# One VectorE instruction for two units: the multiplication by B in a selective scan, 1024 elements against 2048

## What is computed

```
x_dbl = einsum('bld,ed->ble', x, x_proj_w)
delta_r, B, C = x_dbl[..., :128], x_dbl[..., 128:144], x_dbl[..., 144:]
delta = softplus(einsum('blr,dr->bld', delta_r, dt_proj_w) + dt_proj_b)
A = -exp(A_log)
dA  = exp(delta[..., None] * A)                       # 512 channels, 16 states
dBu = (delta * u)[..., None] * B[:, :, None, :]
h   = dA_t * h + dBu_t                                # over 64 tokens, from zero
y_t = einsum('bdn,bn->bd', h, C_t)
y + u * D
```

## Time and profile before

| | |
|---|---|
| median of 3 runs | 1930.55 us (1928.92 to 1934.46) |
| the profiled execution | 1929.09 us, span 1927.3 us |
| VectorE busy | 1456.1 us, 76% of the span |
| TensorE busy | 1832.9 us, 95% |
| GpSimd busy | 1266.2 us, 66% |
| ScalarE busy | 1261.0 us, 65% |
| the scan, L996 | x256, 581.8 us, mean 2273 ns |
| the multiplication by B, L927 | x256, 151.7 + 151.6 us, mean 1194 ns |
| first scan, last scan | 33.5 us, 899.4 us after the span's start |

### The profile page before, as it was taken

The page is one execution under the profiler, slowest core; times in us unless marked ns, Lnnn a source line. Parts: engine busy times, 40 slices in busy tenths (PEclk is TensorE's granted clock), DMA queues, the critical chain, the costliest instruction groups (busy, mean ns, idle before and its releaser), DMA issues.

```text
span 1927.3 us, 30225 instructions
## 1 busy us (share of the span) xinstructions
PE 1832.9 (95%) x9439; PEld 1276.3 (66%) x9439; DVE 1456.1 (76%) x2572; ACT 1261.0 (65%) x3937; POOL 1266.2 (66%) x1251
## 2 busy tenths in 40 slices
PE   6899999999999999988599899999999999999998
PEld 6777777777777777755355575756667575665765
DVE  8999999999999999997545564655657566565522
ACT  5888888888888888765355564655647465564621
POOL 5789999999999999988676554544545454450000
PEclk9999999999999999999799999999999999999999
DMA  5423332333233332321776334334343433431021
GB/s 204 152 105 145 144 117 107 139 145 133 101 128 145 144 122 102 126 88 40 216 213 187 110 102 124 104 107 127 104 119 106 116 109 111 124 91 54 30 71 34
DMA packets 133198, 228.59 MB, mean 119 GB/s; under 512 B 31076, under 2 KB 86388, under 8 KB 128048
## 3 DMA queue, kind: packets, MB, share of 16 engines
q1 hardware_dynamic: 99952, 161.38, 24.0%
q0 software_dynamic: 33088, 65.28, 12.5%
HBM read 209.99 MB, written 44.70 MB: 132 GB/s over the span
## 4 chain that ended last, share of the span: by engine, by line
PE 47%; ACT 2%; issue 1%; DMA 1%; DVE 1%; POOL 0%; DVEq 0%; SPq 0%; ACTq 0%; POOLq 0%
PE attn_psum L1906 12%; PE attn_psum L1922 11%; PE attn_psum L1825 5%; PE attn_psum L1838 5%; PE attn_psum L1818 5%; PE attn_psum L1864 3%; PE attn_psum L1809 2%; PE attn_psum L1940 2%; PE attn_psum L1799 1%; PE attn_psum L1850 1%; ACT xh L1551 1%; ACT th L1552 1%; DMA kv_at<-kv_scratch,new_now 0%; ACT prob L1509 0%; ACT k_t L1499 0%
## 5 line engine op out<-in xcount | busy, mean ns | idle before, releaser
L996 DVE TENSOR_TENSOR_SCAN hid<-scan_psum,dbu 128x1024 f32<-128x1024 f32 x256 | 581.8, 2273 | 0.0
L1161 PE MATMUL scan_psum<-hid,ident 128*128 128x256 f32 x2048 | 519.8, 384 | 28.8 <-POOL hid L492 28.6
L1161 PEld LDWEIGHTS scan_psum<-hid,ident 128*128 128x128 f32 x2048 | 377.9, 190 | 192.0 <-issue 106.4
L1660 DVE CUSTOM_DVE_ANT_0 prob<-attn_psum,mask 128x336 f32<-128x336 f32 x256 | 120.1, 505 | 287.2 <-PE attn_psum L1818 286.8
L492 POOL TENSOR_TENSOR hid<-hid,kv_at 128x1024 f32<-128x1024 f32 x128 | 306.2, 2405 | 27.5 <-DVE hid L996 27.1
L492 POOL TENSOR_TENSOR hid<-hid,bc 128x1024 f32<-128x1024 f32 x128 | 306.0, 2403 | 23.1 <-DVE hid L996 22.8
L1515 ACT COPY p_t<-attn_psum 112x384 f32<-112x384 f32 x256 | 122.3, 484 | 291.6 <-PE attn_psum L1825 291.6
L1922 PE MATMUL attn_psum<-w,ffn_hid 128*128 128x512 f32 x512 | 238.9, 596 | 5.0 <-DVE y_sb L1725 5.0
L1443 POOL DMA_INDIRECT kv_at<-kv_scratch,new_now x189 | 200.5, 1061 | 64.1 <-issue 57.1
L1906 PE MATMUL attn_psum<-xs_in,w 128*128 128x256 f32 x1024 | 232.6, 381 | 7.5 <-ACT xs_in L1521 6.6
L635 ACT ACTIVATE scan_psum<-kv_at,neg_a 128x252 f32<-128x252 f32 x512 | 211.6, 465 | 13.9 <-DVE hid L996 12.3
(11 more groups left out here) (221 smaller groups left out, 3038.7 us busy)
## 6 DMA issues: line engine op xcount, KB each, us to landing
bc<-bc_scratch SPq DMA_DIRECT2D x16, 2048.0 KB, 7.5
kv_at<-bc_scratch SPq DMA_DIRECT2D x15, 2048.0 KB, 7.2
q_scratch<-qg SPq DMA_DIRECT2D x32, 260.0 KB, 2.0
early<-q_scratch SPq DMA_DIRECT2D x32, 260.0 KB, 3.1
x_pair<-in_x_pairs SPq DMA_DIRECT2D x32, 256.0 KB, 2.7
kv_scratch<-kvg SPq DMA_DIRECT2D x32, 256.0 KB, 2.1
a_scratch<-a_sb SPq DMA_DIRECT2D x32, 256.0 KB, 3.4
w_o<-x_scratch SPq DMA_DIRECT2D x32, 256.0 KB, 3.2
```

The source lines that it names most:

```text
L996: nc.vector.tensor_tensor_scan(hid[:, k % RING, :, :].rearrange("p n t -> p (n t)"), decay[k % 2], dbu[:, k % RING, :, :].rearrange("p n t ...
L1161: mm = nc.tensor.matmul(yc, ident[:], hid[:, k % RING, i, :], start=False, stop=(k % 4 == 3 and i == 3))
```

## The change

`times_b` takes a number of units, two by default: one instruction multiplies `du` by the B of 8 states, 2048 elements in each partition, into two neighbouring buffers of the ring. The first two units of all still have an instruction each. In a quarter the order on VectorE becomes: scan 0, multiplication 2 and 3, scan 1, scan 2, multiplication 4 and 5, scan 3, scan 4, multiplication 6 and 7, scan 5, `prepare`, scan 6, multiplication 0 and 1 of the next quarter, scan 7.

```diff
-            def times_b(t, h, q, k):
+            def times_b(t, h, q, k, units=2):
...
-                wait(dve, dve_h, e + 1 - RING)
-                nc.vector.tensor_tensor(dbu[:, k % RING, :, :], du[:, c % 2, :].unsqueeze(1).to_broadcast([P, 4, SUB]),
-                                        bc[q // 2][:, 4 * j:4 * j + 4, 0, :], ALU.mult).then_inc(dve_dbu, 1)
+                wait(dve, dve_h, e + units - RING)
+                nc.vector.tensor_tensor(
+                    dbu[:, k % RING:k % RING + units, :, :].rearrange("p r n t -> p (r n) t"),
+                    du[:, c % 2, :].unsqueeze(1).to_broadcast([P, 4 * units, SUB]),
+                    bc[q // 2][:, 4 * j:4 * (j + units), 0, :], ALU.mult).then_inc(dve_dbu, units)
...
                 for k in range(8):
+                    if k == 6 and parts.next_scan:
+                        prepare(*after)
+                    if s == 0 and k == 0:
+                        times_b(t, h, q, 1, 1)
+                    if k % 2 and k < 7 and parts.scan:
+                        times_b(t, h, q, k + 1)
                     if k == 7 and parts.next_scan:
-                        prepare(*after)
-                    if k < 7 and parts.scan:
-                        times_b(t, h, q, k + 1)
+                        times_b(*after, 0)
...
-                    if k == 7 and parts.next_scan:
-                        times_b(*after, 0)
...
-            times_b(0, 0, 0, 0)
+            times_b(0, 0, 0, 0, 1)
```

## The result

| | before | changed |
|---|---|---|
| median | 1930.92 us, 19 runs | 1935.95 us, 19 runs |
| lowest to highest | 1928.79 to 1934.46 | 1933.11 to 1938.21 |
| changed over before | | 1.0023, 95% interval 1.0016 to 1.0029 |
| the profiled execution's span | 1927.3 us | 1933.8 us |
| first and last scan start | 33.5, 899.4 us | 33.7, 903.4 us |

What follows compares the result with a forecast made beforehand. VectorE and a chain through GpSimd, TensorE and ScalarE were both taken as critical. Terms +5.4, −1.3, −0.15 and +0.9 sum to +4.85; 1930.55 + 4.8 gives 1935.3 us, range 1929.5 to 1939.5.

Steps and rivals of the forecast that it cites:

- the case that was forecast: Scan stage: GpSimd, TensorE and ScalarE delay scan 0 in every second quarter; 1935.3 us, own range 1932.5 to 1938, chance 0.65.
- The sum of 4.85: Whole kernel: +5.4 for twelve pairs of quarters, −1.3 and −0.15 for other quarters, +0.9 for the second quarter.
- The merge: VectorE: a merged multiplication of 2048 elements occupies 2.18 us instead of 2.24, 7.0 us less work over 127 instructions.
- rivals B: VectorE's multiplications: the chain binds and merging saves nothing, spacing 2.23; 1938.8 us, chance 0.10.
- C: VectorE's multiplications: the fixed part is the whole 0.12 us, spacing 2.11; 1930.8 us, no change, chance 0.10.
- The chain: From scan 5 through GpSimd, TensorE and ScalarE to scan 0 two quarters on: 0.56 us later, +0.45 per two quarters.
- The stall of unit 6: Before scan 6: its exponentials come behind `add_bias`, some 0.7 us later, stalling VectorE by up to 0.3, not counted.
- The second quarter: `prepare` waits 3.78 us for GpSimd's `step`, which stands behind unit 5; one-time cost +0.9 us.
- The sentence that what lies behind the scans only starts later: Stages behind the scans: they start later and are unchanged, no cost of their own.
- Rival A: Scan stage: the chain does not bind, under 53.8 us in two quarters, VectorE's saving comes through; 1924.7 us, chance 0.12.
- Rival D: `prepare` meets GpSimd at work in every quarter, up to 2.17 us each; 1993 us, chance 0.03.

Runs made afterwards that it cites:

- order only: Changed kernel with each merged multiplication split into two single ones of 1024 elements, new order kept: 1938.40 us, 1.0037 of the kernel before.
- the tables: Changed kernel with GpSimd's two key tables behind unit 4 instead of unit 5: 1932.34 us, 1.0005 of the kernel before.
- the lock: Changed kernel with `prepare` reading delta alone, without the multiplication by u: 1931.52 us, 1.0002 of the kernel before.
- the copy of q: Changed kernel with ScalarE's exponentials of the next quarter's unit 0 ahead of its copy of q: 1933.24 us, 1.0007 of the kernel before.
- tables and exponentials moved: Changed kernel with key tables behind unit 4 and exponentials of unit 0 ahead of ScalarE's q copy: 1931.26 us, 0.9997 of the kernel before.
- the old order with nearly the same edits: Kernel before with key tables behind unit 4 (to 28th quarter), unit 0's exponentials before q copy, early quarters' second `step` behind unit 3: 1927.40 us.

## Why the prediction was right

The ratio, 1.0023, or 4.5 us, is close to the forecast loss of 4.8, and the case that was forecast is the one that came, by its own rows. That the totals are so close is in part luck. The sum of 4.85 was all in the scan stage, and there the loss was 3.9. Outside it, in the two profiles, stood 0.9 that the prediction had put at nothing: 0.2 ahead of the first scan and 0.7 between the last scan and the first matmul of the attention stage.

- **The merge.** 2.18 per merged instruction, as worked out; rivals B (2.23) and C (2.11) are out. Between order only and the changed kernel the scan stage differs by 4.2 us.
- **The chain.** Two quarters 54.66 expected, 54.60 measured in the pair shown; GpSimd's unit 6 ends 0.56 later expected, 0.52 measured. The difference is one term: the two key tables were taken at 0.28 + 0.32 = 0.60, the last one with its duration, and occupy 524.16 − 523.61 = 0.55. The twelve pairs together gave 4.9 instead of 5.4. The wait is split: 0.51 before scan 0, where 0.6 to 0.9 was expected, and the rest before scan 6. That it is this chain and not another is shown by three edits at three places of it: the tables (0.44 less in a pair), the lock (0.34) and the copy of q (0.17). In the kernel before, where this chain still ends ahead of scan 0, the first and the last of these bring nothing in full quarters.
- **The stall of unit 6.** Expected up to 0.3 and not counted; 0.16 to 0.23 is there, in the quarter that waits anyway.
- **The second quarter.** +0.9 expected; the quarter takes 30.66 instead of 29.74. `prepare` stood 3.71 (3.78).
- **Left out.** The third quarter saved 0.53 instead of 0.22. Two groups are caught up in the third quarter as well, not in the second alone, and `step` stands behind unit 5 there too: before the change `prepare` met it and took 0.98 instead of 0.67, and I had not looked at it. The sentence that what lies behind the scans only starts later is not quite right: GpSimd ends its last unit 9.8 us behind the start of the last scan, before it was 9.1, since it runs later against VectorE throughout. That is the 0.7 above.
- **Rival A** failed as stated: the chain took 54.60, not under 53.8. With tables and exponentials moved it takes 53.97, and there about half of VectorE's saving of 0.44 in a pair comes through. **Rival D** never occurred: `prepare` takes 0.67 in the full quarters, and GpSimd was idle 0.65 ahead of it.
- My own range for the likeliest case was 1932.5 to 1938, and "no change" within 0.3% had the most weight. By that measure it is no change; the interval is narrow enough to say that the small loss is real.

What stays open is a few us of the total. Behind the first matmul of the attention stage the profiled executions take 990.7 us before and 992.4 changed, and 990.7 to 991.9 in the experiments, in no relation to the edits. That no edit touched this stage was only argued; one profile of each kernel can't separate it from scatter, which is 5.7 us between the lowest and the highest of 19 runs of the kernel before. Part of that scatter goes with TensorE's clock. In the rounds of the experiments the kernel before took 1932.8 us on average in the 37 runs with a mean granted clock of 0.987 or less, and 1930.4 in the 32 with more. No run of it with so low a clock was profiled, so where its clock was down is not known.

## What to carry to other kernels

When the busiest engine shows no idle time, look for the chain that ends just ahead of its waits before taking work off it: here the exponentials ended 0.15 us ahead of scan 0, behind a chain of 32 us through three engines, so a saving of 0.22 us in a quarter had nowhere to go in the quarters that this chain reaches. Moving an instruction on the bound engine moves the start of every such chain; list for each engine which item it picks up after idling, and ask what it must do behind the new one. By the scan stage the same saving paid once the neighbours had been reordered into their own idle time (858.8 us, against 862.9 for the old order with nearly the same edits), and each reordering showed where the chain binds next. And before setting two profiles against each other, look at where each execution stands among its kernel's runs, by time and by clock.

## What the runs showed of the hardware

- A VectorE instruction with two inputs in SBUF, of 0.67 us, that starts 0.16 ahead of a GpSimd multiplication makes it 0.36 longer; one of the same length with one input does not (2.72 against 2.36). The multiplication with du in PSUM and B in SBUF, 2048 elements long, leaves GpSimd's units at a median of 2.36 wherever it runs beside them. Met by GpSimd first, `prepare` is held to the end of GpSimd's instruction: it started at 83.82 and took 2.84, up to 86.66, and this one, from the timeline of GpSimd before, ended at 86.10:

```profile
83.75 2.35 POOL L492 TENSOR_TENSOR hid<-hid,kv_at 128x1024 f32<-128x1024 f32 x1
```

  The Trainium skill ("SBUF — State Buffer", the section on two separate sides) says that of a VectorE instruction with two SBUF inputs and a GpSimd one that reads SBUF, the first to start locks the other out for its whole length. The runs agree in both orders.
- TensorE's clock can fall inside a stage that is otherwise full: behind idle times of 1.86 to 2.37 us the matmuls of the last quarters ran at 1.2 GHz in some executions. But in others, or a quarter later in the same one, it stayed at 2.4 GHz behind 1.92, 2.04, 2.13 and 2.22. With early tables a quarter with a fall took 27.8 us instead of 26.87.
- Two scans in a row last 4.46 us together, so about 2.20 from start to start, the same as from a scan to a multiplication.
